# Tent and last gather: no clears of a spare tile between GpSimd's indirect DMAs

## What is computed

```python
# layer 3 (tent)
basis = (bu[:, :, None] * bv[:, None, :]).reshape(-1, k1 * k2)
xj = x[edge_index[1]]
for k in range(k1 * k2):
    msg = msg + basis[:, k:k + 1] * (xj @ w2[k])
out = segment_sum(msg, edge_index[0])
...
# layer 4, its last convolution (spline)
new_pseudo = clip(pseudo + t[col] - t[row], 0.0, 1.0)
basis2, idx2 = spline_basis(new_pseudo)
z = einsum('ni,kio->nko', x, W).reshape(N * K, Fout)
gathered = z[col[:, None] * K + idx2]
msg = einsum('es,eso->eo', basis2, gathered)
out = segment_sum(msg, row) / max(degree, 1) + b
```

## Time and profile before

| | |
|---|---|
| time, median of 3 runs | 11105.01 us (11079.76 to 11107.9) |
| the profiled execution | 11048.03 us, span 11046.2 us |
| busy: PE, DVE, ACT, POOL | 5027.9, 6242.1, 3760.4, 6344.8 us |
| tent, first gather to the end of the last | 8209.4 to 9447.0 us of the span |
| spline, first gather to the end of the last | 9811.6 to 11009.0 us of the span |

### The profile page before, as it was taken

The page is one execution under the profiler, slowest core; times in us unless marked ns, Lnnn a source line. Parts: engine busy times, 40 slices in busy tenths (PEclk is TensorE's granted clock), DMA queues, the critical chain, the costliest instruction groups (busy, mean ns, idle before and its releaser), DMA issues. The chain is left out here.

```text
span 11046.2 us, 132934 instructions
## 1 busy us (share of the span) xinstructions
PE 5027.9 (46%) x27720; PEld 4148.1 (38%) x27721; DVE 6242.1 (57%) x14299; ACT 3760.4 (34%) x7451; POOL 6344.8 (57%) x7840
## 2 busy tenths in 40 slices
PE   4232244443556666543333266666643334653323
PEld 2111133333534444333333266666623334333323
DVE  6454465555331111158888788888754444555655
ACT  0000023222123333234444377777643333331111
POOL 3767666766035555547777344444327777137776
PEclk8556555565566766655555555555565555875555
DMA  6332222222455555547777799999722222787776
GB/s 199 110 110 76 61 58 60 62 57 55 158 159 191 196 185 194 152 131 198 209 206 208 204 348 347 354 348 351 270 103 70 68 68 64 257 302 226 228 229 198
DMA packets 998183, 1952.73 MB, mean 177 GB/s; under 512 B 537330, under 2 KB 537639, under 8 KB 980184
## 3 DMA queue, kind: packets, MB, share of 16 engines
q0 software_dynamic: 317952, 1023.05, 29.1%
q1 hardware_dynamic: 613464, 790.12, 21.9%
q10 hardware_dynamic: 66688, 138.68, 3.7%
HBM read 1341.33 MB, written 612.99 MB: 177 GB/s over the span
## 5 line engine op out<-in xcount | busy, mean ns | idle before, releaser
L1771 POOL DMA_INDIRECT got<-node_rows,now x1664 | 1765.2, 1061 | 1449.1 <-issue 878.6
L1771 POOL DMA_INDIRECT got<-corners,now x1664 | 1608.0, 966 | 1661.0 <-issue 839.2
L1771 POOL DMA_INDIRECT got<-patches,now x832 | 814.7, 979 | 581.9 <-issue 292.8
L948 POOL DMA_INDIRECT d_rows<-row x832 | 836.2, 1005 | 466.8 <-issue 456.4
L1677 PE MATMUL made_p<-weights,turned 64*128 64x320 f32 x2450 | 778.1, 639 | 552.0 <-issue 274.9
L2704 PE MATMUL sum_p<-msg_s,hot_s 128*128 128x64 f32 x3328 | 737.3, 423 | 595.6 <-DVE msg_s L2093 595.6
L699 POOL DMA_INDIRECT s_rows<-row_now,pos_i x784 | 758.0, 967 | 365.8 <-issue 356.2
L2704 PEld LDWEIGHTS sum_p<-msg_s,hot_s 128*128 128x128 f32 x3328 | 717.7, 332 | 604.6 <-DVE msg_s L2093 604.6
L1819 DVE TENSOR_TENSOR a<-a,sum_p 128x64 f32 x832 | 183.5, 220 | 1220.9 <-remote 680.7
L1701 ACT COPY z<-made_p 128x384 f32<-128x384 f32 x1225 | 524.8, 489 | 951.3 <-DMA d_rows<-row 508.2
L1677 PEld LDWEIGHTS made_p<-weights,turned 64*128 64x128 f32 x2450 | 453.0, 260 | 812.2 <-issue 406.2
(11 more groups left out here) (405 smaller groups left out, 12955.2 us busy)
## 6 DMA issues: line engine op xcount, KB each, us to landing
corners<-z SPq DMA_DIRECT2D x245, 960.0 KB
over<-logits SPq DMA_DIRECT2D x104, 1024.0 KB
corners<-z SPq DMA_DIRECT2D x98, 864.0 KB
d_rows<-empty ACTq DMA_DIRECT2D x32, 1586.0 KB
row<-d_rows SPq DMA_DIRECT2D x104, 488.0 KB
corners<-z SPq DMA_DIRECT2D x49, 672.0 KB
s_rows<-empty ACTq DMA_DIRECT2D x32, 962.0 KB
row<-s_rows SPq DMA_DIRECT2D x104, 296.0 KB
```

Of the source, the lines that this page charges most:

```text
L948: pool.indirect_dma_start(out=d_rows, out_offset=bass.IndirectOffsetOnAxis(ap=to[:, t, DPOS:DPOS + 1], axis=0), in_=row[b][:, t, :], in_of ...
L1771: pool.indirect_dma_start(out=to[b][:, t, :], out_offset=None, in_=table, in_offset=bass.IndirectOffsetOnAxis(ap=indices.now[b][:, t:t + 1 ...
```

## The change

Two of the five stages that clear the spare tile no longer do so: in `tent_phase` and `spline_phase` the object is not made, and `gather` is called without it. Gone with the clears are the semaphore that counts them, the wait on it, and the two increments around that wait. What is gathered, and the waits for indices, for sums and for landings, stay as they were.

```diff
 def tent_phase
-        spare = Spare(k, ph)
...
-                spare.begin(pool)
...
                         if b == 0:
                             pool.wait_ge(summed, i * 4 + 2)
                             pool.sem_inc(seen, 1)
-                        gather(pool, got, table, indices, i, b, gathered, spare=spare)
+                        gather(pool, got, table, indices, i, b, gathered)
 def spline_phase
-        spare = Spare(k, ph)
...
-                spare.begin(pool)
...
-                        gather(pool, got, conv.table, indices, i, b, gathered, spare=spare)
+                        gather(pool, got, conv.table, indices, i, b, gathered)
```

## The result

The changed kernel takes 11159.78 us (median of 7 runs, 11129.1 to 11195.33), the kernel before 11095.04 us (median of 7, 11044.76 to 11107.9). The ratio is 1.0059, 95% interval 1.0036 to 1.0083: slower by 65 us where 105 us less were forecast.

A forecast was written before the change was run, and what follows sets the result against it. No engine bounds the whole; in tent and spline, POOL issues or waits for PE's sums. Terms -58 - 58 + 12 = -105 us gave 10943 us against the profiled execution, 11000 from the median; range 10850 to 11150.

The forecast's parts named there:

- A pair of gathers: Tent and spline stages, POOL: a pair falls from 2.64 to 2.50 us, saving 58 us per stage, 117 together.
- The semaphore instructions: Tent and spline stages: four instructions leave per half group, hidden behind queued gathers; taken as 0, at most 101 us.
- The pauses at the start of a quad: POOL's long tent and spline waits needn't depend on gather time; 12 us loss taken, bounds 219 gained to 186 lost.
- Port contention: Tent stage: gathers lengthened beside DVE's two-SBUF-operand work, 22 us becoming some 23; the 1 us was left out.
- Transfers keep up: Spline stage: 227 GB/s at DMA share 0.75 becomes 240 and 0.79, so transfers do not limit.
- Pauses take it back: Rival, tent and spline quads: POOL stops 2.2 us sooner and waits 2.2 longer; 11105 us within 30; chance 0.16.
- Slow stretches spread: Rival, tent and spline: denser gathers bring PE's slow stretch earlier, POOL waits longer; +69 us, 11175; chance 0.13.
- Pauses vanish: Rival, tent and spline: clears and semaphores slow PE, so removing them gains a further 219 us at most, 10780; chance 0.10.
- Gathers get longer: Rival, tent and spline: gathers lengthen without clears, losing 337 us and gaining 117; +220, 11325; chance 0.05.
- 1145 us for the spline window: Sign to check in the profile after: the spline stage's window should be 1145 us long, beside 1179 for tent.

The follow-up runs named there:

- counts_only: Kernel before with the tent and spline clears' memsets dropped, semaphore increments and waits kept; 9993.41 us against 10104.31, ratio 0.9891.
- counts_third: Tent and spline memsets dropped, semaphore increments and waits kept, against the kernel before at 11102.03 us; 11151.53 us, ratio 1.0063.
- spline_only: Kernel before with only the spline stage's clears removed, tent clears kept; 10049.22 us against 10104.31, ratio 0.9943.
- after_again: The changed kernel itself timed again, against the kernel before at 10079.36 us; 9973.03 us, ratio 0.9893.
- tent_only: Kernel before with only the tent stage's clears removed, spline clears kept; 10042.3 us against 10104.31, ratio 0.9945.
- noise_third: Changed kernel plus 9600 semaphore increments on otherwise idle SP in the spline stage, against the kernel before at 11102.03 us; 11605.23 us, ratio 1.0472.

## Why the prediction was wrong, step by step

*A pair of gathers, 0.14 us saved.* Right. The run of a tent quad went from 43.3 to 40.1 us, 3.1 us, of which 16 pairs are 2.2 and the rest shorter gathers (23.6/26 = 0.9). In the 10.1 ms sessions the two stages gave 111 and 106 us, where the term said 117.

*The semaphore instructions, nothing.* Right at both levels: counts_only 0.9891 beside 0.9893; counts_third has quads of 50.0 and 46.1 us, like the change itself, and 1.0063 [1.0038, 1.0088] beside 1.0047 and 1.0059. The prediction counts four instructions that leave per half group; the traces have 1250 fewer over 416 half groups, so three.

*The pauses at the start of a quad, +12 us.* This is the step that failed. The 12 us had the right sign, since denser gathers were to bring PE's slow stretches a little sooner; but the text took the pause for independent of the gathers. It said that a pause is "the time from POOL's stop to PE's recovery plus 1.4 us", so that its "length needn't depend on how long the gathers before took". It does depend on it. The pauses grew by 189 us (136 tent, 53 spline), just past the bound of 186 that the text kept for the worst case. With the 117 us saved and the 23.6 us of shorter gathers that makes +48, where the two stages measured +53. What the runs showed in place of the step: in such sessions a spline quad takes 46.1 us whatever POOL saves, and in the tent stage PE has more left to do when POOL stops (28.8 passes of a quad instead of 10.8). The evidence for a fixed rate was in view: in the trace before, each of the spline stage's quads of 42.3 us without a pause was followed by one of 49 to 51 us, and I took the first alone as a sign that quads can be short.

*Port contention, left out.* Mis-sized: the tent stage's long gathers, put at +1 us, fell by 23.6. They lie beside DVE's work, and the reading is that DVE now does much of it while POOL pauses, so that this is an effect of the pauses and no gain of its own. The 10.1 ms session bears it out: without pauses the tent stage's gathers take 961 ns with the clears (spline_only) and 962 without (after_again).

*Transfers keep up.* Right: 259 GB/s at a share of 0.85 in the 10.1 ms session, where the stage took 1046 us (240 and 0.79 were forecast for 1139 us), and 228 at 0.74 in the 11.1 ms session, where the fixed rate holds them.

*The rivals.* "Pauses take it back" (0.16) is what the spline stage did: -6 us. "Slow stretches spread" (0.13) is what the tent stage did, +59. The second was to decide from a mean pause of 6.4 us on; it was (10.1 + 6.0)/2 = 8.1. Its time, 11175, is 15 us from the result. Both rivals were named with what would decide them, and the chances put on them were low. "Pauses vanish" had the sign of the clears' effect wrong: without them the pauses grew, and counts_third, which keeps the semaphore work and drops only the clears' time, has the long quads too. So it is the time between gathers that counts, not the semaphores. "Gathers get longer" did not occur (951 and 945 ns). One sign was written down inconsistently: 1145 us for the spline window, where the prediction's own terms give 1197.4 - 58 + 12 = 1151.

The cause of the level stays open. Shown: it goes with the session and not with the chip; about 950 of the 1000 us lie in the five stages that have the clears, counting the trace before against tent_only and spline_only in the stages that these leave as they were, while of the two without clears message lasts 1694 to 1697 us everywhere and score 1293 to 1318 us at the lower level and 1314 to 1359 at the upper; it slows what PE's and SP's sequencers do beside them and not the gathers. Shown too: the trace itself has lost records there. It holds 157186 semaphore updates of the changed kernel in the 10.1 ms session and 64551 here, though all 130852 instructions and 998195 packets are there at both levels. Even the message stage, as long at both levels, has 15171 updates against 21774 (before, and tent_only). Two causes can be set aside by the traces. The fetching of instructions is not it: its queues moved one packet in the whole spline stage of the changed kernel at either level. Slower transfers are not it either: the packets of the spline gathers took 213 and 214 ns on the mean.
The Trainium skill ("NOTIFIC — the notification-queue block", Overflow: three behaviours, one of which stalls the engine) says that the block which writes instruction and semaphore records holds its producers back when it is full inside, so that recording itself can stall an engine. By that rule the level would be how fast the host takes the records, and part of the 1000 us a price of being measured. The same page (Constraints, capacities, measured rates) reports no overflow at 6.6 million records a second, 6.6 per us, and did not reach a ceiling. The 10.1 ms trace of the changed kernel holds 157186 updates and 130852 instructions in 9963 us, 29 per us, and its quads have no pauses.
Against a plain limit on the number of these records stands this: the 11.1 ms trace of the changed kernel holds 42 of them per us around 3000 us, as the 10.1 ms trace does in the same code, and noise_third holds 32.5 per us once its gathers are over. The changed kernel's spline stage holds 9 per us with pauses, and the same stage at the 10.1 ms level 21 without. So if recording is the cause, something of the gathers must take part in it. That recording is the cause is argued and not shown: every run here was recorded, and a run without recording wasn't tried.

## What to carry to other kernels

Take an engine that issues work and pauses for a consumer at regular places. Measure the length of a whole period, run and pause together, over several kernels or quads before pricing a faster run; if periods agree while runs differ, the run is not the bound. Instructions that look useless between dense DMAs can be spacing: their price is their own time where nothing else limits, and the pause they prevent where something does, and which holds should be measured in more than one session. When a change in one session loses and the same kernel wins in the next, compare the unchanged kernel across sessions first.

## What was not expected of the hardware

- The same program on the same chip took 10079 us in one session and 11102 in another (chip 13), 10104 and 11257 (chip 15), and the sign of the change turns with it: 0.9893 and 1.0059, no clears at all 0.9718 and 1.0101.
- At the upper level an idle engine's sequencer is held too: SP's semaphore increments fall from 16.0 to 1.75 per us beside dense gathers (noise_third).
- A clear of 128x192 fp32 behind a gather costs 0.14 us of its 0.277, because the idle gap ahead of the next gather is 0.16 us behind a clear and 0.30 us behind a gather: 111 and 106 us for 832 of them removed.
- Twice as many clears in five stages (4112 for 2056), and wider ones, made the program 3.5% faster at the upper level.
